# GpSimd's split of expert weights, moved behind VectorE's last operation of each weight tile, with a third buffer from unit ten

## The reference, cut to what matters

```python
x = x + L0_ffn(L0_cond(x))     # 2048 tokens of 512 numbers, in float32
x = x + L1_ffn(L1_cond(x))
# L0_ffn: k = 0, 1 are the two chosen ranks of a router with 8 experts
base1 = x @ W1.T + b1                          # W1 (2048, 512)
h = gelu(base1 + z1_k @ B1_rf * SCALING)
y = h @ W2.T + b2 + z2_k @ B2_rf * SCALING
res = res + w_topk[:, k:k + 1] * y
# L1_ffn: a shared expert (704 wide) and 8 routed ones (352 wide, top 2)
g = silu(x @ w_gate[e]) * (x @ w_up[e]);  routed += comb[e] * (g @ w_down[e])
```

## Time and profile before

| | us |
|---|---|
| median of 3 runs | 1057.41 |
| profiled execution, its own time | 1054.48 |
| its span, first to last instruction | 1052.9 |
| TensorE busy in the span | 1009.4 |
| VectorE busy | 597.3 |
| GpSimd busy | 389.3 |
| first and last store of the units issued at | 172.8 and 516.7 |

### The profile page before, as it was taken

How to read it: one execution, slowest core, us unless ns; L and a number is a source line. 1 busy time by engine, 2 the same in 40 slices (tenths; PEclk the granted TensorE clock), 3 DMA queues, 4 the chain that set the end, 5 groups by cost and what they waited for, 6 DMA issues and landing times.

```text
span 1052.9 us, 14889 instructions
## 1 busy us (share of the span) xinstructions
PE 1009.4 (96%) x4894; PEld 834.4 (79%) x4895; DVE 597.3 (57%) x905; ACT 260.5 (25%) x433; POOL 389.3 (37%) x411
## 2 busy tenths in 40 slices
PE   8899999999999899899999999999999999999995
PEld 5678887778877688677776778777889999999994
DVE  3888778678596787857767442475362222222221
ACT  3743322111121112111233211120113333332221
POOL 4334433555654565545324100003113333333332
PEclk9999999999999999999999999999999999999998
DMA  7387545878868788697645210100664786786843
GB/s 237 133 301 275 173 153 171 291 240 295 296 219 298 242 292 297 219 344 247 244 138 198 82 40 1 40 1 1 222 250 77 234 240 174 249 238 166 247 72 40
DMA packets 65197, 202.04 MB, mean 192 GB/s; under 512 B 9812, under 2 KB 11108, under 8 KB 64644
## 3 DMA queue, kind: packets, MB, share of 16 engines
q1 hardware_dynamic: 41476, 124.21, 35.0%
q0 software_dynamic: 21488, 75.26, 23.9%
q10 hardware_dynamic: 2192, 2.08, 0.7%
HBM read 129.42 MB, written 72.10 MB: 191 GB/s over the span
## 4 chain that ended last, share of the span: by engine, by line
PE 79%; DVE 14%; DMA 2%; ACT 2%; issue 1%; ACTq 1%; PEldq 0%; POOLq 0%; PEld 0%; DVEq 0%
PE ps_y L1749 5%; PE ps_y L1751 4%; PE ps_y L1750 4%; PE ps_h L1707 4%; PE ps_h L1708 4%; PE ps_h L1709 4%; DVE g_lo L1236 3%; PE ps_y L2018 3%; PE ps_y L2022 3%; PE ps_y L2017 3%; PE ps_h L1997 2%; PE ps_y L1992 2%; PE ps_h L1993 2%; PE ps_y L1997 2%; PE ps_y L1993 2%; PE ps_h L1992 2%
## 5 line engine op out<-in xcount | busy, mean ns | idle before, releaser
L1749 PE MATMUL ps_y<-w_hi,g_hi 128*128 (+1 forms) x256 | 103.8, 405 | 18.3 <-DVE g_lo L1236 18.3
L818 POOL DMA_INDIRECT out_x<-yt,slot_tok x39 | 61.6, 1580 | 157.3 <-DMA out_x<-yt,slot_tok 110.6
L1596 DVE TENSOR_TENSOR rgt_lo<-ps_u,rgt_hi 128x384 fp32r<-128x384 f32 x39 | 21.7, 557 | 166.5 <-ACT rgt_hi L1052 166.5
L1228 DVE TENSOR_TENSOR h<-h,wb 128x512 f32<-128x512 f32 x64 | 51.6, 806 | 105.4 <-ACT h L939 103.6
L933 ACT ACTIVATE h<-ps_h,bias 128x512 f32<-128x512 f32 x64 | 44.0, 689 | 238.5 <-PE ps_h L1716 238.5
L1707 PE MATMUL ps_h<-xt_hi,w_hl 128*128 128x512 f32 x256 | 100.2, 391 | 1.3 <-ACT lg_t L882 0.7
L1750 PE MATMUL ps_y<-w_lo,g_hi 128*128 (+1 forms) x256 | 101.2, 395 | 0.0
L1751 PE MATMUL ps_y<-w_hi,g_lo 128*128 (+1 forms) x256 | 101.1, 395 | 0.0
L1709 PE MATMUL ps_h<-xt_hi,w_hl 128*128 128x512 f32 x256 | 100.3, 392 | 0.0
L1708 PE MATMUL ps_h<-xt_lo,w_hl 128*128 128x512 f32 x256 | 100.2, 391 | 0.0
L1241 DVE TENSOR_TENSOR g_lo<-h,g_hi 128x512 fp32r<-128x512 f32 x64 | 79.6, 1244 | 2.2
(11 more groups left out here) (323 smaller groups left out, 2472.9 us busy)
## 6 DMA issues: line engine op xcount, KB each, us to landing
w_hl<-w1s_d SPq DMA_DIRECT2D x49, 704.0 KB, 4.6
e_d<-pre_hi POOLq DMA_DIRECT2D x42, 384.0 KB, 4.4
w1s_d<-w_hl SPq DMA_DIRECT2D x16, 704.0 KB, 6.1
eg_hi<-e_d SPq DMA_DIRECT2D x7, 1408.0 KB
eg_lo<-e_d SPq DMA_DIRECT2D x7, 1408.0 KB
w_raw<-in_w1b SPq DMA_DIRECT2D x16, 608.0 KB, 5.3
pre_raw<-in_we POOLq DMA_DIRECT2D x21, 384.0 KB, 5.9
u1t<-in_we POOLq DMA_DIRECT2D x21, 384.0 KB, 5.6
```

Of the source, the lines that this page charges most:

```text
L818: pool.indirect_dma_start(out=out, in_=yt[t % 4][:], in_offset=None, out_offset=bass.IndirectOffsetOnAxis(ap=slot_tok[:, t:t + 1], axis=0) ...
L1228: tt(h1[u][:], h1[u][:], wb[:, v, :], ALU.mult).then_inc(gch, 1)
L1749: mm(ps_y[:, j, :], g_hi[u][:, cols], sl(w2_hi), start=first, **kw)
```

## The change

The units are taken apart and put in a new order, the subtractions are tied to VectorE's progress, and a third raw buffer is added.

- `low_unit(k)` now waits for `g1_done` of tile 18 + k (the end of L1241 of that tile). The copy of unit k + 1 follows at once, then the low store of unit k, the high store of unit k + 1, and then the next load or loads.
- `load_unit(0)` and `load_unit(1)` are issued at the start; the copy of unit 0 waits for `g1_done` of tile 17.
- In iteration k up to 7 the load is that of unit k + 2, into the buffer that unit k has just used, so GpSimd's queue waits there for unit k's low store to land. From iteration 7 on it is that of unit k + 3: units 0 to 7 use buffers 0 and 1 in turn, units 8 to 41 use 0, 1, 2 in turn. The third buffer is columns 768 to 1535 of `u1t`; it is first filled with unit 10, after a wait for `z_ok` of 6. From unit 8 on a load waits for the low store of the unit three before it.
- The waits for the end of the stores cover three buffers, and one such wait is added on GpSimd ahead of `low_s(1)`.

```diff
+    IN_TWO = 8
+    raw_of = [k % 2 if k < IN_TWO else (k - IN_TWO) % 3 for k in range(AHEAD)]
+    raw_used = [raw_of[:k].count(raw_of[k]) for k in range(AHEAD)]
...
-        pre_raw = [sb_ahead("pre_raw0", [P, UW])[:], u1t[:, 0:UW]]
+        pre_raw = [sb_ahead("pre_raw0", [P, UW])[:], u1t[:, 0:UW], u1t[:, UW:2 * UW]]
...
             def load_unit(k):
-                u = k % 2
-                pool.wait_ge(d_done, 2 + FT + max(k - 1, 0))
-                if k >= 2:
-                    pool.wait_ge(pre_lo_st[u], 16 * (k // 2))
+                u = raw_of[k]
+                if k < 2:
+                    pool.wait_ge(d_done, 2 + FT)
+                if u == 2 and not raw_used[k]:
+                    pool.wait_ge(z_ok, 6)
+                if raw_used[k]:
+                    pool.wait_ge(pre_lo_st[u], 16 * raw_used[k])
                 at = k % UNITS * UW
                 pool.dma_start(pre_raw[u], we1[k // UNITS, :, at:at + UW]).then_inc(pre_in[u], 16)
 
             def high_unit(k):
-                u = k % 2
-                pool.wait_ge(pre_in[u], 16 * (k // 2 + 1))
+                pool.wait_ge(pre_in[raw_of[k]], 16 * (raw_used[k] + 1))
                 if k >= 2:
-                    pool.wait_ge(pre_hi_st[u], 16 * (k // 2))
-                nc.gpsimd.tensor_copy(pre_hi[u], pre_raw[u]).then_inc(pre_hi_done, 1)
+                    pool.wait_ge(pre_hi_st[k % 2], 16 * (k // 2))
+                nc.gpsimd.tensor_copy(pre_hi[k % 2], pre_raw[raw_of[k]]).then_inc(pre_hi_done, 1)
+
+            def store_high(k):
                 pool.wait_ge(pre_hi_done, k + 1)
-                pool.dma_start(e_d[k // UNITS, 0, k % UNITS], pre_hi[u].bitcast(F32)).then_inc(pre_hi_st[u], 16)
+                pool.dma_start(e_d[k // UNITS, 0, k % UNITS], pre_hi[k % 2].bitcast(F32))\
+                    .then_inc(pre_hi_st[k % 2], 16)
 
             def low_unit(k):
-                raw = pre_raw[k % 2]
+                raw = pre_raw[raw_of[k]]
+                pool.wait_ge(g1_done, 2 + FT + 3 + k)
                 nc.gpsimd.tensor_tensor(raw.bitcast(F32R), raw, pre_hi[k % 2].bitcast(F32), ALU.subtract)\
                     .then_inc(pre_lo_done, 1)
+
+            def store_low(k):
                 pool.wait_ge(pre_lo_done, k + 1)
-                pool.dma_start(e_d[k // UNITS, 1, k % UNITS], raw).then_inc(pre_lo_st[k % 2], 16)
+                pool.dma_start(e_d[k // UNITS, 1, k % UNITS], pre_raw[raw_of[k]]).then_inc(pre_lo_st[raw_of[k]], 16)
 
             def units(ks):
                 for k in ks:
-                    high_unit(k)
+                    low_unit(k)
                     if k + 1 < AHEAD:
-                        load_unit(k + 1)
-                    low_unit(k)
+                        high_unit(k + 1)
+                    store_low(k)
+                    if k + 1 < AHEAD:
+                        store_high(k + 1)
+                    if k < IN_TWO:
+                        load_unit(k + 2)
+                    if IN_TWO - 1 <= k < AHEAD - 3:
+                        load_unit(k + 3)
 
             shared_at = (NS - 2) * FT + 2
             load_unit(0)
+            load_unit(1)
+            pool.wait_ge(g1_done, 2 + FT + 2)
+            high_unit(0)
+            store_high(0)
             units(range(shared_at))
...
                 if n == 1:
                     pool.wait_ge(a_done, STEPS)
+                    for u in range(3):
+                        pool.wait_ge(pre_lo_st[u], 16 * raw_of.count(u))
...
                     for u in range(2):
                         dve.wait_ge(pre_hi_st[u], 16 * (AHEAD // 2))
-                    for u in range(2):
-                        dve.wait_ge(pre_lo_st[u], 16 * (AHEAD // 2))
+                    for u in range(3):
+                        dve.wait_ge(pre_lo_st[u], 16 * raw_of.count(u))
```

More of the change, by code:

```diff
@@ L347, in adaln_ffn @@
         out_st = sem("out_st")
-        pre_in = [sem(f"pre_in{u}") for u in range(2)]
+        pre_in = [sem(f"pre_in{u}") for u in range(3)]
         pre_hi_done = sem("pre_hi_done")
@@ L351, in adaln_ffn @@
         pre_hi_st = [sem(f"pre_hi_st{u}") for u in range(2)]
-        pre_lo_st = [sem(f"pre_lo_st{u}") for u in range(2)]
+        pre_lo_st = [sem(f"pre_lo_st{u}") for u in range(3)]
         half_in = sem("half_in")
@@ L643, in _ @@
                 sp.wait_ge(pre_hi_st[u], 16 * (AHEAD // 2))
-            for u in range(2):
-                sp.wait_ge(pre_lo_st[u], 16 * (AHEAD // 2))
+            for u in range(3):
+                sp.wait_ge(pre_lo_st[u], 16 * raw_of.count(u))
             sp.wait_ge(gu_done, NS * SH)
```

## The result

The changed kernel takes 1077.03 us, the median of 4 runs (1076.41 to 1079.29), beside 1058.84 for the kernel before (4 runs). The ratio is 1.0207 (95%: 1.0170 to 1.0245): slower. The ratio makes that some 22 us of 1057, with 18 to 26 in its interval; the two medians lie 18.2 us apart. The forecast was 1069.8, with a range of 1044 to 1085. The profiled execution took 1076.41, its span 1074.8, which is 21.9 us above the profiled execution of the kernel before.

The account below looks back on a forecast made before the run. TensorE, busy 96% of the span, bounds the kernel, with 18.3 us of waits for VectorE's L1236. 11.8 - 1.4 + 2 = 12.4 us on the span's 1054.48 gives 1066.9, plus 2.9 to the median: 1069.8, range 1044 to 1085.

Parts of the forecast that it names:

- the 12.4 us: Net loss summed at the end of the unit stream: 11.8 late, minus 1.4 slack, plus 2 for `low_s(1)`.
- GpSimd's queue waits for its own low store: Units on GpSimd: each load issue stands until the low store issued just before has landed, making GpSimd late.
- The rival in which the stream keeps up: GpSimd gets on time, s below 4.0 with three buffers: minus 10 to 15 us, about 1044; chance 0.25.
- Cycle with two buffers: Early units: copy, low store landing and load landing follow in full, 10.75 us; GpSimd 27 us late at unit 9.
- the 4.7 that I took for s: Time in us from a low store's issue to its landing, taken between 4.0 and 5.5.
- Cycle with three buffers: Units 10 to 41: queue waits at each load for the low store just issued; 3.37 + s, or 8.07 us.
- What this costs: End of the stream: VectorE waits at `low_s(0)` until 551.3, tile 62 starts 11.8 us late; sum 12.4 us.
- the 2 us for GpSimd's `low_s(1)`: Added loss as `low_s(1)` runs beside tile 62's chain: counted as 2 us, between 0 and 3.24.
- What it saves in the steps before counts for nothing: Steps before the stream's end: savings left out, since the end of the stream sets the end of the stage.
- that sentence: GpSimd's cycle near 8 us drifts along VectorE's chain; where TensorE's step is stretched, the two can keep pace awhile.
- the clock's share: TensorE idling tens of us at one place could lower its clock; at half speed each us of matmuls costs another half.
- the upper tail: GpSimd late and slower still, s = 5.5, three-buffer cycle 8.87 us: about 1105; chance 0.07 for all above 1085.

Follow-up runs that it names:

- e9: Changed kernel with low store between subtraction and copy, load of unit k + 2 ending each iteration, shared loads behind units 36 and 38: 1042.63 us.
- e1: Changed kernel with GpSimd's copy (from unit 2) and subtraction cut from 768 to 32 columns, all transfers and waits kept: 1039.76 us.
- e8: Kernel before the change with GpSimd's copy (from unit 2) and subtraction cut to 32 columns: 1037.97 us.
- e10: e9 without the subtraction's wait for VectorE's last operation of the tile (L1264): 1061.49 us.
- e4: Changed kernel without the subtraction's wait for VectorE's L1264, the copy of unit 0 keeping its own: 1082.60 us.
- e3: Changed kernel with the low store issued between the subtraction and the next copy: 1067.38 us.
- e5: Changed kernel with low store between subtraction and copy, and the load of unit k + 2 at the end of every iteration: 1046.82 us.

## Why the prediction was right and where it was wrong

The sign and the range held, but by luck: the 12.4 us were summed at a place where nothing was lost, and the loss came from steps that the sum counted as nothing.

**Right: GpSimd's queue waits for its own low store.** All 39 such loads did, and GpSimd was late in 37 of 42 units. The rival in which the stream keeps up is out, and it named the right price for a stream that keeps up: 10 to 15 us to gain; e9, where it does, gained 13 to 14.

**Cycle with two buffers: sized too long.** I took 0.85 + 4.7 + 5.2 = 10.75 us. The copies of units 2 to 9 start from 202.67 to 263.40, 8.68 apart in the mean. In that stretch the high store behind the low one slowed it little: low stores landed after 2.9 us in the median, loads after 3.6, as the view of the two lines from 190 to 258 us says (low stores, then loads):
```profile
DMA to landing us min/median/max: 2.7/2.9/4.7
...
DMA to landing us min/median/max: 3.5/3.6/5.2
```
By the Trainium skill, DMA: Bandwidth & Descriptors, section Anatomy of one DMA, 384 KB come to about 2.9 us (an estimate); the low stores of this stretch agree with it, the loads, at 3.6, do not. From 258 us on the low stores have a median of 3.9 and a longest of 7.7, so it is no figure for the crowded part, where the case is decided. Their mean over units 9 to 38 is 4.9, so the 4.7 that I took for s was nearly right. The rival asked for s under 4.0, and a median of 3.9 did not make the stream keep up: a cycle that is repeated some 30 times adds up means, not medians.

**Cycle with three buffers: sized too short.** I took 8.07; it was 8.6 (subtraction of unit 9 at 267.69, of unit 41 at 541.19, 273.5 / 32 = 8.55 with the shared loads in it). Stores that fall just behind SyncE's weight load keep the queue for 5.0 to 8.0 us, but that is in the mean of 4.9 above and explains 0.2 of the 0.5. Three waits for VectorE's gate, which the sum had at nothing, are in it too: 4.13, 3.42 and 1.75 us at units 14, 30 and 41. The first two stand behind the longer pieces between super tiles, where GpSimd had caught up. The two errors mostly cancel, again by luck: the last subtraction was forecast at 546.3 and started at 541.2.

**Wrong: "What this costs".** I let VectorE wait at `low_s(0)` until the last store had landed, and counted 11.8 us of 12.4 there. There was no wait at all; VectorE came to it at 557.36, 13.6 us behind the last store's issue. The longest wait of TensorE there was 3.59 us, not some 10, and the 2 us for GpSimd's `low_s(1)` were not lost either.

**Wrong, and the step that failed: "What it saves in the steps before counts for nothing".** I treated the steps as free of loss because the end of the stream sets the end of the stage, and priced GpSimd's falling on the chain by the earlier trace rows as before: 1 us, now and then. It was the loss, as far as e1 and e8 can tell. Two sizes were missing. The old order put two DMA issues, and mostly a wait, between copy and subtraction, so one VectorE operation met one of the two; in the new order it meets both, up to 3.55 us instead of 2.70. VectorE's slack of 1.40 us covers only half of an added 2.8. And a late GpSimd with a cycle of 8.6 beside a step of 7.4 does not drift through the chain but stays on it, since each collision stretches the step towards 8.6 (the 13 steps from tile 34 to 47 took 8.48 us in the mean, 7.82 before; this reading is argued from the timeline); I had written that sentence and not priced it. By e1 and e8 the blocking costs 37 us after and 19 before.

**Too small: the clock's share.** I left it to the upper tail. At tile 59 TensorE stood still for 3.59 us, and the matmuls behind it came 0.43 us apart instead of 0.23 until 545.90, 14 of them, some 2.7 us.

The sum was 12.4 us; the ratio gives 21.9, the medians 18.2.

## What to carry to other kernels

Tying an operation to another engine's progress pays only when its queue can be on time, and then it pays all it promises (18.9 us in e10 against e9, nothing clear in e4 against the change). So look at what stands ahead of the tied operation in its queue: a wait for a transfer issued a moment ago belongs behind an iteration of other work. Price a late background engine by each step it collides with, not by when its stream ends, and leave a gap between two of its operations when another engine has to get in between.

## What the runs showed of the hardware

- A VectorE operation caught by a GpSimd operation is not let in when the next GpSimd operation follows at once: 3.27 us in place of 0.43 for L1257, over two GpSimd operations of 1.84 and 0.82. With the store's issue between them (e3, e5) no chain operation took over 2.9 us. By the Trainium skill, SBUF — State Buffer, section "SBUF: two separate sides", the shared port pair is an exclusive lock that the first comer holds for a whole instruction while the other blocks fully. The trace agrees that one of the two stands until the other is over, 2.70 us in the earlier trace rows. It does not agree on the first comer: by the profile's starts VectorE's L1236 came 0.30 us before GpSimd's L723 in the earlier trace rows, and L1257 0.37 us before L732 here, and each time VectorE was the one blocked; nor does the blocking end with the first GpSimd operation here.
- Behind a stop of 3.59 us TensorE's granted clock was 0.50 from 540 to 544 us, its 1.2 GHz level, and 0.72 from 544 to 548:
```profile
540.00:544.00 4.00, 3.80 (x9) 3.04 (x10) 3.97 (x5) 0.00 (x0) 2.51 (x2) 0.50 0.36 144
544.00:548.00 4.00, 4.00 (x14) 3.16 (x14) 2.18 (x5) 1.94 (x2) 0.32 (x1) 0.72 0.24 98
```
- The same 384 KB store kept GpSimd's queue for 2.9 us or for 8.0, by where it fell behind another queue's 704 KB load. That the load is the cause is argued from the timeline only; no run moved it.
